# Two low-rank products of neighbouring blocks turned by one transposition, in five of eight token pairs

## The reference

```python
x = x + einsum('bct,bcd->bdt', x, w0[idx])                          # _L0
x = x + x @ W1 + (x @ A1[idx]) @ B1[idx]                            # _L1, rank 16
x = x + x @ W2.T + (x @ A2[lab]) @ B2.T * 0.5                       # _L2, rank 32
logits = x @ Wr.T + 5 * one_hot(language)                           # _L3
gates = sum of one_hot(topi) * softmax(top 2 of logits)
x = x + x @ W3.T + 2 * einsum('bter,bte,eor->bto', x @ A3, gates, B3)  # 8 experts of rank 16
```

## Time and profile before

| | |
|---|---|
| median of three runs | 521.19 us (520.95 to 521.24) |
| the profiled execution's own time | 521.43 us |
| its span, first to last instruction | 519.6 us |
| busy in the span: TensorE, DVE, ACT, POOL | 515.1, 334.2, 201.9, 170.2 us |
| granted TensorE clock | full in every slice |
| pairs 2 to 6 of the loop (counted from 0) | 314.5 to 485.2 us, 34.14 us each |

### The profile page before, as it was taken

How to read it: one execution, slowest core, us unless ns; L and a number is a source line. 1 busy time by engine, 2 the same in 40 slices (tenths; PEclk the granted TensorE clock), 3 DMA queues, 4 the chain that set the end, 5 groups by cost and what they waited for, 6 DMA issues and landing times.

```text
span 519.6 us, 8870 instructions
## 1 busy us (share of the span) xinstructions
PE 515.1 (99%) x2720; PEld 450.4 (87%) x2720; DVE 334.2 (64%) x655; ACT 201.9 (39%) x351; POOL 170.2 (33%) x250
## 2 busy tenths in 40 slices
PE   8999999999999999999999999999999999999997
PEld 8999999988988888888887888888888888888886
DVE  4798886799533333399876864756647557476464
ACT  5744653345222222267344233323333333233322
POOL 2550000002102020219546544354254434552400
PEclk9999999999999999999999999999999999999999
DMA  7911210214430202040703303313233042222312
GB/s 263 374 65 40 60 40 1 82 40 125 158 112 0 82 0 82 0 166 4 242 2 118 121 23 119 100 47 108 83 117 121 34 117 86 69 87 81 120 32 81
DMA packets 29631, 46.80 MB, mean 90 GB/s; under 512 B 12052, under 2 KB 17940, under 8 KB 29476
## 3 DMA queue, kind: packets, MB, share of 16 engines
q1 hardware_dynamic: 29268, 45.72, 27.3%
q0 software_dynamic: 192, 0.59, 0.3%
q10 hardware_dynamic: 144, 0.13, 0.1%
HBM read 33.39 MB, written 13.04 MB: 89 GB/s over the span
## 4 chain that ended last, share of the span: by engine, by line
PE 98%; DVE 1%; ACT 0%; issue 0%; POOL 0%; POOLq 0%; DVEq 0%; ACTq 0%
PE bank L1893 26%; PE bank L1827 15%; PE bank L1759 11%; PE bank L1882 8%; PE bank L1801 6%; PE bank L1730 5%; PE bank L1813 5%; PE bank L1973 4%; PE bank L1941 4%; PE bank L1949 4%; PE bank L1714 3%; PE bank L1944 1%; PE bank L1943 1%; PE bank L1903 1%; PE bank L1721 1%; PE bank L1930 0%
## 5 line engine op out<-in xcount | busy, mean ns | idle before, releaser
L1893 PE MATMUL bank<-t_hi,em_hi 128*128 128x512 f32 x168 | 57.3, 403 | 0.0
L1183 DVE TENSOR_TENSOR w1t_lo<-raw,w1t_hi 128x1024 fp32r<-128x1024 f32 x18 | 24.1, 1339 | 23.6 <-ACT w1t_hi L909 17.1
L684 POOL TENSOR_TENSOR tmp<-raw 128x512 f32<-128x512 f32 x4 | 7.2, 1793 | 97.2 <-DVE raw L1369 97.2
L1893 PEld LDWEIGHTS bank<-t_hi,em_hi 128*128 128x128 f32 x168 | 31.1, 188 | 7.2 <-DVE em_hi L1183 0.4
L1827 PE MATMUL bank<-te,em_hi 128*128 128x512 f32 x144 | 34.9, 395 | 0.0
L1827 PEld LDWEIGHTS bank<-te,em_hi 128*128 128x128 f32 x144 | 27.0, 188 | 6.6
L670 POOL CAST em_hi<-tba 128x256 fp32r x32 | 13.4, 447 | 58.3 <-PE bank L1882 54.6
L1183 DVE TENSOR_TENSOR em_hi<-tmp,em_hi 128x512 fp32r<-128x512 f32 x22 | 15.1, 688 | 21.7 <-ACT em_hi L1016 12.6
L674 POOL TENSOR_TENSOR em_lo<-tba,em_hi 128x256 fp32r<-128x256 f32 x32 | 27.1, 868 | 2.4 <-POOL em_hi L670 1.2
L1759 PE MATMUL bank<-em_hi,w2s_hi 128*128 128x384 f32 x80 | 27.0, 337 | 0.0
L1759 PE MATMUL bank<-em_lo,w2s_hi 128*128 128x384 f32 x80 | 26.9, 337 | 0.0
(11 more groups left out here) (309 smaller groups left out, 1615.2 us busy)
## 6 DMA issues: line engine op xcount, KB each, us to landing
raw<-in_x_dram SPq DMA_DIRECT2D x16, 512.0 KB, 4.2
b1s<-b1scr SPq DMA_DIRECT2D x32, 217.5 KB, 2.8
raw<-in_b1w_dram SPq DMA_DIRECT2D x10, 512.0 KB, 3.6
out_dram<-ef SPq DMA_DIRECT2D x16, 256.0 KB, 2.1
out_dram<-ost SPq DMA_DIRECT2D x15, 256.0 KB, 2.5
graw<-in_w3a3wr_dram SPq DMA_DIRECT2D x4, 768.0 KB, 11.0
b1scr<-b1stage SPq DMA_DIRECT2D x12, 256.0 KB
w2raw<-in_w_dram SPq DMA_DIRECT2D x6, 384.0 KB, 6.8
```

The lines of the kernel that those rows point to most:

```text
L1183: V.tensor_tensor(dst, src, f32(hi), ALU.subtract).then_inc(signal, 1)
L1893: ins = nc.tensor.matmul(to[:, :], left[a][:, k0 + k, :], m_right(right, z, k), start=(name in OPENS and n == 0), stop=(n == 3 * KH - 1), ...
```

## The change

It concerns pairs 2 to 6, which get loops of their own (`skewed_pair_products`, `skewed_pair_lo`, `skewed_pair_hi`); pairs 0, 1 and 7 keep their code.

- h2 of the first block (64 columns: hi, lo) and h1 of the second block (64 columns: hi, lo for two batch rows) are written side by side in one tile h21c of 128 columns and turned by one transposition, `h21_across`, within p7. The first block's `h2_across` in p6 and the second block's `h1_across` in p7 go.
- ACT copies the turned halves to their places in h1T and h2T, repeated thirds and quarters being written from the same rows: five copies (`h21_t`) where there were two.
- To lie together, the layouts change: h1's three thirds stand as (hi, lo, hi) with the two batch rows interleaved, the thirds in the scratch copy b1scr are stored as (hi, hi, lo), and the rows of b1s lie on every second partition.
- The first block's `h2_into` moves from p6 to p3, its `route` on DVE behind the second block's `second_low_rank`, its `gates` behind `left_lo` (the next pair's first operand), its `gated_across` into the next narrow product (behind 18 of its 24 matmuls).
- The second block's `route` and `gates` follow: `gates` stands behind `xn_lo` of the next pair's first block and ahead of `xm_lo` of tile 2; it waits for the first block's `gated_across`, since gh is one buffer. Its `gated_across` stands behind tile 1, `ght_hi` behind `xm_hi` of tile 3, `ght_lo` behind `xm_lo` of tile 3 and ahead of `ost_odd` of tile 1.

```diff
+    H2_COLS, H1_COLS = 2 * R2, 2 * PER * R1
+    assert H2_COLS + H1_COLS == P == E * R3
+    h21c = at("h21c", [P, P], F32R, at_gh + 4 * (E * R3 - H2_COLS))
...
+    H1_THREE = h1c[:, :].rearrange("p (t r h) -> p t r h", t=3, h=PER)
+    H2_NEXT = h21c[:, 0:H2_COLS].rearrange("p (z r) -> p z r", z=2)
+    H1_NEXT = h21c[:, H2_COLS:P].rearrange("p (z r h) -> p z r h", z=2, h=PER)
...
-                    for third, half in enumerate((0, 1, 0)):
+                    for third, half in enumerate((0, 0, 1)):
...
-                    rows = slice(h * SEG1, (h + 1) * SEG1)
+                    rows = slice(h, PER * SEG1, PER)
...
+            def h21_t(p):
+                act.wait_ge(s_th, skewed_turns(p) + 2)
+                turned = bank[RT]
+                nc.scalar.activation(h1T[1][0:H1_COLS, :], turned[H2_COLS:P, Z2], ACT.Copy).then_inc(s_hts, 1)
+                nc.scalar.activation(h1T[1][H1_COLS:2 * SEG1, :], turned[H2_COLS:H2_COLS + PER * R1, Z2], ACT.Copy).then_inc(s_hts, 1)
+                nc.scalar.activation(h2T[0][0:R2, :], turned[0:R2, Z2], ACT.Copy).then_inc(s_hts, 1)
+                nc.scalar.activation(h2T[0][R2:2 * R2, :], turned[0:R2, Z2], ACT.Copy).then_inc(s_hts, 1)
+                nc.scalar.activation(h2T[0][2 * R2:SEG2, :], turned[0:H2_COLS, Z2], ACT.Copy).then_inc(s_hts, 1)
...
+            def skewed_pair_hi(p):
+                b0, b1 = 2 * p, 2 * p + 1
+                made = PRODUCTS * p - PRODUCTS
+                act.wait_ge(s_sum, 4 * p - 3)
+                act.wait_ge(s_mix, 4 * p - 1)
+                operand_hi(CS[0], tmp[:, :, :])
+                h1_t_from(skewed_turns(p) + 1, 0)
+                act.wait_ge(s_sum, 4 * p - 2)
+                act.wait_ge(s_st[0], 16 * p)
+                act.wait_ge(s_st[1], 16 * p)
+                operand_hi(DS[0], tmp[:, :, :])
+                held_back(p, "p1", held_p1, bank[BA])
+                act.wait_ge(s_raw[1], 16 * p + 16 * (ROWS // 2 + 1))
+                act.wait_ge(s_mix, 4 * p)
+                act.wait_ge(s_st[2], 16 * p)
+                act.wait_ge(s_st[3], 16 * p)
+                operand_hi(XB[0][:, :, :], raw[1][:, :, :])
+                held_back(p, "p5", held_p5, bank[BC])
+                act.wait_ge(s_sum, 4 * p)
+                operand_hi(CS[0], raw[1][:, 0:KH, :])
+                xn_hi(b1, YB)
+                act.wait_ge(s_sum, 4 * p - 1)
+                operand_hi(XB[0][:, 0:KH, :], tmp[:, :, :])
+                h21_t(p)
+                act.wait_ge(s_wide, made + PRODUCT["p7"])
+                xm_hi(0, bank[BA])
+                h2_t_from(skewed_turns(p) + TURNS, 1)
+                exp_of(b0)
+                left_hi(p + 1)
+                act.wait_ge(s_wide, made + PRODUCT["p3"])
+                xm_hi(1, bank[BD_])
+                exp_of(b1)
+                ght_hi(b0, 0)
+                xn_hi(b0 + 2, YB + 1)
+                act.wait_ge(s_add, 3 * p)
+                act.wait_ge(s_mix, 4 * p + 1)
+                xm_hi(0, bank[BC])
+                ost_even(p, 0)
+                act.wait_ge(s_wide, made + PRODUCT["p4"])
+                act.wait_ge(s_mix, 4 * p + 2)
+                xm_hi(1, bank[BB])
+                ght_hi(b1, 1)
+                ost_even(p, 2)
...
-                    steps.then(V.tensor_copy(h1c[ts, h * SEG1:h * SEG1 + 2 * R1].rearrange("p (m r) -> p m r", m=2),
-                                             nar[ts, at_:at_ + R1].unsqueeze(1).to_broadcast([T, 2, R1])))
+                    steps.then(V.tensor_copy(H1_THREE[ts, 0:3:2, :, h], nar[ts, at_:at_ + R1].unsqueeze(1).to_broadcast([T, 2, R1])))
-                    lo(h1c[ts, h * SEG1 + 2 * R1:(h + 1) * SEG1], nar[ts, at_:at_ + R1], h1c[ts, h * SEG1:h * SEG1 + R1], s_h1c)
+                    lo(H1_THREE[ts, 1, :, h], nar[ts, at_:at_ + R1], H1_THREE[ts, 0, :, h], s_h1c)
...
+            def h1_of_second(p, steps):
+                nar = bank[RT + 1]
+                dve.wait_ge(s_small, 6 * p + SMALL["mixed", 1])
+                for h in range(PER):
+                    ts, at_ = slice(h * T, (h + 1) * T), C3 + PER * R2 + h * R1
+                    steps.then(V.tensor_copy(H1_NEXT[ts, 0, :, h], nar[ts, at_:at_ + R1]))
+                steps.hold()
+                for h in range(PER):
+                    ts, at_ = slice(h * T, (h + 1) * T), C3 + PER * R2 + h * R1
+                    lo(H1_NEXT[ts, 1, :, h], nar[ts, at_:at_ + R1], H1_NEXT[ts, 0, :, h], s_h1c)
+            def h2_of_first(p, steps):
+                nar = bank[RT]
+                dve.wait_ge(s_small, 6 * p + SMALL["h1", 0])
+                for h in range(PER):
+                    ts, at_ = slice(h * T, (h + 1) * T), C3 + h * R2
+                    steps.then(V.tensor_scalar(H2_NEXT[ts, 0, :], nar[ts, at_:at_ + R2], SCALE2, None, ALU.mult))
+                steps.hold()
+                for h in range(PER):
+                    ts, at_ = slice(h * T, (h + 1) * T), C3 + h * R2
+                    V.scalar_tensor_tensor(H2_NEXT[ts, 1, :], nar[ts, at_:at_ + R2], SCALE2, f32(H2_NEXT[ts, 0, :]),
+                                           ALU.mult, ALU.subtract).then_inc(s_h2c, 1)
+            def second_low_rank(b, s, steps, there=None):
                 nar = bank[RT + s]
-                dve.wait_ge(s_small, 3 * b + 2)
+                dve.wait_ge(s_small, 3 * b + 2 if there is None else there)
                 for h in range(PER):
                     ts, at_ = slice(h * T, (h + 1) * T), C3 + h * R2
                     steps.then(V.tensor_scalar(h2c[ts, 0:3, :], nar[ts, at_:at_ + R2].unsqueeze(1).to_broadcast([T, 3, R2]),
...
-            def gates(b, s, steps):
+            def gates(b, s, steps, gh_free=None):
+                if gh_free is not None:
+                    dve.wait_ge(s_tg, gh_free)
...
+            def skewed_pair_lo(p, steps):
+                b0, b1 = 2 * p, 2 * p + 1
+                ops = OPS * p - OPS
+                operand_lo(CS[1], tmp[:, :, :], CS[0], ops + 2)
+                first_low_rank(b0, 0, steps, 6 * p + SMALL["mixed", 0])
+                operand_lo(DS[1], tmp[:, :, :], DS[0], ops + 3)
+                h2_of_first(p, steps)
+                operand_lo(XB[1][:, :, :], raw[1][:, :, :], XB[0][:, :, :], ops + 4)
+                sum_p1(p)
+                operand_lo(CS[1], raw[1][:, 0:KH, :], CS[0], ops + 5)
+                sum_p5(p)
+                xn_lo(b1, YB)
+                operand_lo(XB[1][:, 0:KH, :], tmp[:, :, :], XB[0][:, 0:KH, :], ops + 6)
+                h1_of_second(p, steps)
+                sum_p7(p)
+                second_low_rank(b1, 1, steps, 6 * p + SMALL["h1", 1])
+                route(b0, 0, steps, 6 * p + SMALL["h2", 0])
+                xm_lo(0, bank[BA], 4 * p + 1)
+                left_lo(p + 1)
+                gates(b0, 0, steps)
+                route(b1, 1, steps, 6 * p + SMALL["h2", 1])
+                xm_lo(1, bank[BD_], 4 * p + 2)
+                ght_lo(b0, 0)
+                xn_lo(b0 + 2, YB + 1)
+                gates(b1, 1, steps, b0 + 1)
+                xm_lo(0, bank[BC], 4 * p + 3)
+                xm_lo(1, bank[BB], 4 * p + 4)
+                ght_lo(b1, 1)
+                ost_odd(p, 1)
+                ost_odd(p, 3)
...
+            def narrow(b, left, to, ks=range(K)):
+                if ks.start == 0:
+                    pe.wait_ge(s_sel, 4 * b + 4)
+                    if isinstance(b, int) and b == 0:
+                        pe.wait_ge(s_s0l, 1)
+                    above(pe, s_xnl, b)
+                for k in ks:
+                if ks.stop == K:
...
+            def h21_across(p):
+                pe.wait_ge(s_h2c, 4 * p + 2)
+                pe.wait_ge(s_h1c, 4 * p + 4)
+                nc.tensor.matmul(bank[RT][:, Z2], f32(h21c[:, :]), ident[:, :], is_transpose=True, start=False, stop=True,
+                                 skip_group_check=True).then_inc(s_th, 1)
...
+            def skewed_pair_products(p):
+                b0, b1 = 2 * p, 2 * p + 1
+                ops, sums = OPS * p - OPS, 3 * p - 3
+                copies = skewed_copies(p)
+                part("p1", 0, 5)
+                mixed(b0, 0)
+                part("p1", 5, 11)
+                h1_across(b0, 0)
+                part("p1", 11, 12)
+                pe.wait_ge(s_opl, ops + 2)
+                part("p5", 0, 9)
+                h1_into_from(copies + 1, 0, p)
+                part("p5", 9, 12)
+                pe.wait_ge(s_opl, ops + 3)
+                part("p6", 0, 12)
+                pe.wait_ge(s_opl, ops + 4)
+                narrow(b1, second_block, YB)
+                pe.wait_ge(s_cp, 2 * p - 1)
+                part("p2", 0, 7)
+                mixed(b1, 1)
+                part("p2", 7, 12)
+                pe.wait_ge(s_add, sums + 2)
+                pe.wait_ge(s_opl, ops + 5)
+                part("p7", 0, 9)
+                h21_across(p)
+                part("p7", 9, 12)
+                pe.wait_ge(s_opl, ops + 6)
+                part("p3", 0, 2)
```

(82 more changed lines are left out.)

7 lines of the change are left out of this document (4 added, 3 removed).

## The result

| | |
|---|---|
| median after | 531.54 us (530.49 to 532.01, six runs) |
| median before, same chip | 521.36 us (520.95 to 521.82, six runs) |
| ratio | 1.0192, 95% interval 1.0179 to 1.0205 |
| the profiled execution after | 531.61 us, span 529.8 us, granted clock full |
| pairs 2 to 6 | 35.48, 36.13, 36.38, 36.15, 36.13 us |

The change makes the kernel 1.9% slower: 10.2 us, where 523.9 (2.7 more) was forecast and 525.8 was the top of the range. The sign was right, the size was not. The five pairs carry 9.6 us of the difference: they last 180.27 us together, and 170.70 (5 x 34.14) before.

The account below looks back on a forecast made before the run. TensorE, busy throughout the loop pairs, was taken as the bound. From 521.43 us: -0.55 transpositions, +2.6 tile 2 stall, +0.56 SP's queue, then to the median (523.8), +0.1 left_lo: 523.9 us, range 522.6 to 526.0 (with rivals 521.4 to 525.8).

Parts of the forecast that it names:

- What bounds the kernel: TensorE, busy for all 34.14 us of a loop pair, has no waits to remove; only instructions taken off it shorten the kernel.
- The transposition at 0.11 us: Six transpositions per pair become five on TensorE; each saves 0.11 us by matmul spacing, 0.55 us over five pairs.
- Small edits: Strided h1c, ACT's copies, b1scr order and b1s on every second partition: put at zero cost, b1s landing within 0.3 either way.
- They count once: TensorE's waits at narrow(b1) and the first b1s product share one delay: 0.14 us in four pairs, 0.56 in all.
- ost_odd(1) 0.34 later: DVE's last tail step, on which SP's queue hangs, comes 0.34 us later against the next pair; slack 0.20.
- Gates of b1 under `take`: b1's gates on DVE, slowed by POOL's `take`, delay xm_lo(0); TensorE stalls before tile 2, 0.52 us a pair, 2.6 in all.
- left_lo 0.1: Allowance of 0.1 us for DVE's left_lo, pushed back when x lands late and POOL sums it; range 0 to 0.75.
- Rival D: Besides the gates' clash, late x lets POOL's sum precede left_lo; narrow(b0+2) waits 0.4 a pair: 525.8 us, chance 0.10.
- The sum: Whole kernel: transpositions saved, tile 2 stall, SP's queue and left_lo added to the time before, forecast 523.9 us, 0.5% slower.
- rival C: Nothing waits if b1's gates take under 2.0 us and SP's stores and b1s land 0.3 sooner: 520.6 us, chance 0.12.

Follow-up runs that it names:

- e6: The changed kernel with SP's index loads made before its first store wait and POOL's `take` (not its index loads) held behind b1's gates: 520.86 us, ratio 0.9989.
- e7: The kernel before the change, with only SP's eight index loads of a pair made before it waits for the first store: 521.24 us, ratio 0.9995.
- e2: The changed kernel with the rows of b1s lying together again, so the first low-rank product multiplies wrong rows with the same work: 525.44 us, ratio 1.0069.
- e1: The changed kernel with the old order of steps in every pair, only the layouts new, six transpositions per pair: 524.48 us, ratio 1.0055.
- e5: The changed kernel with SP's eight index loads of a pair made before it waits for the pair's first store: 524.69 us, ratio 1.0066.

## Why the prediction was right in sign and wrong in size

**What bounds the kernel: right.** With no wait on TensorE in the kernel before, the gain could be no more than what left it. e6 and e7 show it from both sides.

**The transposition at 0.11 us: right.** Pairs without a wait last 34.02 to 34.04 us after 34.14. The spacing of the matmuls gave the price; the record of 0.27 would have made 33.87. The Trainium skill's page "TensorE: Matmul & The Clock Gate" (Part 4: PE-mode transpose) gives about 275 ns; that agrees with the record and not with what a pair became shorter by.

**Small edits: the step that failed.** "The rows of b1s on every second partition keep the bytes and the number of DMAs; no row shows what the layout does to their landing, so I allow from 0.3 us sooner to 0.3 later, and take 0." A DMA has two prices, what it takes to land and what it takes its queue to issue, and only the first was bounded. It did not move; the issue went from 0.32 to 0.37 us up to 0.51 to 0.58, eight times in a pair, in a queue whose slack the prediction itself had put at 0.20. So a term that was put at nothing cost 0.8 us per batch of four. The trace of before had no issue of this form, so the row for the four issues (2.04) was the nearest, and it was carried over at its full value where a bound was due. With 0.8 more for four issues, the same step would have given 0.94 a pair (0.34 + 0.8 - 0.20) instead of 0.14, 3.8 us in its four pairs; the two waits took 3.7 there, and 0.7 in pair 2, which the prediction had left out. e2 shows the new order without the price: the queue then costs what was forecast (0.55 after 0.56), and some 6 of the 10.2 us are gone. e1 shows the price without the new order, 2.7 us: the rest comes only where the new order has used the slack up.

**"They count once": right.** The two waits of the queue, for b1s and for narrow(b1), are 2.2 us each, but they share one delay. The store ahead of xb_hi, behind all four issues, is late by 1.10; TensorE, held up by 0.5 at b1s, comes that much later to narrow(b1) and waits there only for what is left, 0.3 to 0.55. In the four pairs that follow a changed one, narrow(b1) starts 0.80 to 1.01 later than in e6, near the 0.94 that counting once gives.

**ost_odd(1) 0.34 later: right within 0.05.** The loads of b1s start 0.30 later.

**Gates of b1 under `take`: right in mechanism, a third too small.** The stall was put at 0.52 a pair. It is 0.50 in pair 2 of the kernel after and about 0.5 in every other pair of e5, but 0.85 to 0.88 in the others. One outcome of a race was read (b0's gates in the earlier trace rows, where gate took 0.66), and taken for the rule; in the kernel before, all five pairs show this one. In its other outcome both gm wait and the gates last 2.88 instead of 2.52. The term was 2.6 and measured 4.0. The Trainium skill's page "SBUF — State Buffer" (Who interferes with whom) says that the order of issue decides which of the two blocks. The rows of e5 neither confirm nor deny the order: the same seven instructions have two outcomes 0.36 us apart, though gm's record begins 0.10 us ahead of POOL's in both. With POOL moved away (e6) neither outcome is there.

**left_lo 0.1: too small.** Rival D's mechanism came, as a consequence of the queue: x is issued 1.7 later instead of D's 0.34, POOL's sum starts ahead of left_lo, and narrow(b0+2) waits up to 0.5 us (1.3 with what lies before it). In e5, where x is early, it is gone.

**The sum.** Forecast: -0.55 + 2.6 + 0.56 + 0.1 = +2.7. Measured in the profiled execution: -0.55, +4.0 at tile 2, +4.4 and 0.44 (last pair) behind the queue, +1.3 at narrow(b0+2), +0.5 elsewhere: +10.1 of 10.2. Of rival C's conditions e6 shows what it would take: gates away from `take`, and a queue with slack. Its time of 520.6 lies 0.3 below e6's.

What stays open: why an issue to every second partition takes longer, and what decides the race under `take`. Steps of one and of two partitions were compared, with runs of 48 rows; no other step and no other count of rows was tried, nor a layout in which the rows lie in three runs.

## What to carry to other kernels

A DMA whose layout changes has to be priced twice, for its landing and for its issue; when the issues of a serial queue come ahead of stores and loads that a saturated engine waits for, the issue is the one that can count, and its price adds up over all issues ahead. The same long issues cost nothing once the queue had slack (e5), and less where it had some (e1): two small delays that share one slack have to be added before they are held against it. Where two engines race for a resource, a trace can show one outcome only, here in all five pairs of the kernel before: allow for the other order before carrying a length over. Before a wait is put ahead of a step to move it, look at what the step's arguments do: here the index loads of the moved step, 3 us, went along, and only with these left in place did the move pay.

## What the runs showed of the hardware that was not expected

- SP's issue of a load to 48 SBUF partitions takes 0.51 to 0.58 us when they are every second one (one of 64 took 1.21) and 0.32 to 0.37 when they are neighbours, for 6 KB as for 217.5 KB; the time to landing is the same or shorter (2.8 us for both layouts with the large loads; 2.3 against 2.6 with the small).
- DVE instructions of 128x8 elements under POOL's two subtractions: the two gm take 0.92 or 1.58 us instead of 0.48, gate 0.66 or 0.38 instead of 0.17, and which of them is hit changes from pair to pair.
- Four of five pauses of TensorE of 2.4 us in an otherwise full stretch were followed by a drop of the clock (in pair 4 matmul steps of 0.42 instead of 0.23 us, in pair 3 a granted clock of 0.72 over 3.5 us); the fifth, of the same length, left it at 1.00.
